# Masked attention on one Trainium2 core: key group 4 moves from TensorE's transposes to the second DMA transpose

## What is computed

```python
q, k, v = x @ Wq.T + bq, x @ Wk.T + bk, x @ Wv.T + bv
scores = q @ k.T / sqrt(128)
scores = where(adj > 0, scores, -9e15)        # adj: int32 [4096, 4096]
att = softmax(scores, axis=-1) @ v
y = x + elu(att)
out = (y - mean(y)) / sqrt(var(y) + 1e-5)
```

## Time and profile before

| | us |
|---|---|
| median of 3 runs | 428.43 (428.37 to 428.65) |
| profiled execution | 429.13 |
| its span in the profile | 427.3 |

### The profile page before, as it was taken

One profiled execution on the slowest core, in us unless ns is written; L12 is line 12 of the kernel. 1 busy time (PEld: TensorE's weight loads), 2 busy tenths in 40 slices (PEclk: granted clock), 3 DMA queues, 4 the chain that ended last, 5 costly groups with the idle time before them and its releaser, 6 DMA issues.

```text
span 427.3 us, 11462 instructions
## 1 busy us (share of the span) xinstructions
PE 416.2 (97%) x3470; PEld 311.3 (73%) x3470; DVE 360.8 (84%) x677; ACT 353.8 (83%) x742; POOL 354.0 (83%) x644
## 2 busy tenths in 40 slices
PE   7997999999999999999999999999999999999994
PEld 6764777767777777777777777777777777777784
DVE  3889988888888898888888988888889888888784
ACT  4987788888888889888888898888888988888892
POOL 0596578988898889888988898889888988898875
PEclk9999999999999999999999999999999999999999
DMA  8944999899999999999999999999999999998550
GB/s 253 399 161 111 266 275 251 208 294 263 286 268 254 275 264 267 238 280 266 259 251 280 268 265 244 272 271 263 245 277 271 256 250 271 263 267 225 104 103 21
DMA packets 149794, 104.77 MB, mean 245 GB/s; under 512 B 132755, under 2 KB 141461, under 8 KB 141717
## 3 DMA queue, kind: packets, MB, share of 16 engines
q1 hardware_dynamic: 149344, 104.41, 92.0%
q10 hardware_dynamic: 436, 0.20, 0.2%
HBM read 69.47 MB, written 2.10 MB: 167 GB/s over the span
## 4 chain that ended last, share of the span: by engine, by line
POOL 58%; issue 18%; PE 10%; DMA 4%; ACT 3%; DVE 2%; POOLq 2%; SPq 2%; ACTq 0%; DVEq 0%
POOL p_rows L409 26%; POOL res L423 5%; POOL var_eps L445 4%; POOL rstd L447 4%; POOL att_sum L416 3%; POOL y L428 3%; POOL neg_mean L434 3%; POOL att L418 3%; POOL centred L436 2%; POOL expm L425 2%; DMA p_turned<-p_rows 2%; PE ps_out L967 2%; POOL y_out L451 2%; DMA x_rows<-in_x_dram 2%; POOL var L443 1%
## 5 line engine op out<-in xcount | busy, mean ns | idle before, releaser
L409 POOL TENSOR_TENSOR p_rows<-scores,p_rows 128x256 f16<-128x256 f32 x252 | 177.0, 733 | 7.3 <-ACT p_rows L566 7.1
L696 DVE CUSTOM_DVE_ANT_0 scores<-ps_scores,adj 128x1024 f32<-128x1024 f32 x128 | 155.9, 1218 | 13.0 <-issue 9.3
L549 ACT ACTIVATE scores<-scores,neg_max 128x1024 f32<-128x1024 f32 x128 | 145.8, 1139 | 3.5 <-DVE neg_max L706 3.5
L712 DVE TENSOR_TENSOR p_lo<-ps_t,p_hi 128x512 f16<-128x512 f32 x124 | 82.6, 686 | 28.4 <-ACT p_hi L558 28.3
L682 DVE TENSOR_SCALAR adj<-adj 128x1024 f32<-128x1024 int32 x128 | 103.5, 810 | 0.2
L928 PE MATMUL ps_scores<-k_hi,q_hi 128*128 128x512 f16 x256 | 97.0, 379 | 0.5 <-DVE max_parts L696 0.5
L929 PE MATMUL ps_scores<-k_lo,q_hi 128*128 128x512 f16 x256 | 97.0, 379 | 0.0
L930 PE MATMUL ps_scores<-k_hi,q_lo 128*128 128x512 f16 x256 | 97.0, 379 | 0.0
L967 PE MATMUL ps_out<-v_parts,p_turned 128*128 128x256 f16 x496 | 95.0, 273 | 0.4 <-DMA p_turned<-p_rows 0.3
L967 PE MATMUL ps_out<-v_parts,p_hi 128*128 128x256 f16 x496 | 95.1, 273 | 0.0
L969 PE MATMUL ps_out<-v_parts,p_lo 128*128 128x128 f16 x496 | 88.5, 219 | 0.0
(11 more groups left out here) (121 smaller groups left out, 479.8 us busy)
## 6 DMA issues: line engine op xcount, KB each, us to landing
adj<-in_adj_dram SPq DMA_DIRECT2D x63, 1024.0 KB, 5.3
out_dram<-y_out SPq DMA_DIRECT2D x32, 64.0 KB, 4.9
x_rows<-in_x_dram SPq DMA_DIRECT2D x4, 256.0 KB, 4.4
x_rows<-in_x_dram SPq DMA_DIRECT2D x2, 512.0 KB, 7.6
adj<-in_adj_dram SPq DMA_DIRECT2D x2, 512.0 KB, 7.4
p_turned<-p_rows SPq DMA_TRANSPOSE x63, 4.5
w_rows<-in_L_gnn_Wq_dram ACTq DMA_DIRECT2D x1, 64.0 KB, 2.7
w_rows<-in_L_gnn_Wk_dram ACTq DMA_DIRECT2D x1, 64.0 KB, 3.3
```

What stands on the lines that cost most here:

```text
L409: last = nc.gpsimd.tensor_tensor(p_rows[c][:, w:][:, cols], s_sb[s][:, c * PIECE:c * PIECE + w][:, cols], p_rows[c][:, 0:w][:, cols], ALU. ...
L549: nc.scalar.activation(s_sb[s][:, cols], s_sb[s][:, cols], ACT.Exp, bias=neg_max[:, s:s + 1], accum_out=p_sums[:, s, c:c + 1]).then_inc(ex ...
L696: nc.vector.tensor_tensor_reduce(out=s_sb[s][:, cols], in0=ps_scores[c % 2][:, :], in1=mask_sb[s][:, cols], scale=SCALE, scalar=-3.0e38, o ...
L712: nc.vector.tensor_tensor(p_lo[:, k, :], ps_t[bank_of(s, g)][:, :], p_hi[:, k, :], ALU.subtract).then_inc(plo_ready, 1)
```

## The change

`DMA_COLS` becomes (PIECE, PIECE + BANK), so the second turn also holds group 4, with 3072 columns, and PE transposes groups 5 to 7. The high part of group 4 is a copy of its own on ACT (`high_rows_odd`, at j = 6), and its low part is made by VectorE (`low_rows_odd`, at j = 7 behind `row_max`), not by POOL. `turn` of c = 1 waits for both low parts. `high_rows` of piece 1 goes from j = 6 to j = 4. `PV_ORDER` becomes (5, 0, 1, 6, 7, 2, 3, 4). The masks are made two pieces ahead: pieces 2 and 3 of a tile at its own j = 1 and 3, pieces 0 and 1 of the next at j = 5 and 7. SP's order of DMAs stays. The rest fits prologue and epilogue to it. Cut to its core (semaphores and index changes of the last tile are left out where there is "..."):

```diff
--- before.py
+++ after.py
@@ -18,12 +18,12 @@
 EPS = 1e-5
 LOG_P_SCALE = 15.0 * math.log(2.0)
-DMA_COLS = (PIECE, PIECE)
+DMA_COLS = (PIECE, PIECE + BANK)
 BY_DMA = len(DMA_COLS)
 FIRST_PE = sum(DMA_COLS) // BANK
 PE_GROUPS = STEPS - FIRST_PE
-T_AT = {4: 6, 5: 7, 6: 8, 7: 10}
-PV_ORDER = (4, 0, 5, 6, 1, 7, 2, 3)
+T_AT = {5: 6, 6: 8, 7: 10}
+PV_ORDER = (5, 0, 1, 6, 7, 2, 3, 4)
 Q_AT = (4, 6, 7, 8, 10, 11, 12)
...
@@ -274,18 +276,26 @@
         last_ps = dict(zip(range(LAST_PE, STEPS), last_ps + [ps_t[0][:, :], ps_t[1][:, :]]))
+        LAST_ACT = 4
+
+        def turned_parts(g, s):
+
+            c = 0 if g < 2 else 1
+            first = (g - 2 * c) * BLOCKS
+            half = DMA_COLS[c] // P
+            return (p_turned[c][s][:, first:first + BLOCKS, :], p_turned[c][s][:, half + first:half + first + BLOCKS, :])
+
         def last_high(g):
             if g >= FIRST_PE:
                 return p_hi[:, g - FIRST_PE, :]
-            return p_turned[g // 2][1][:, g % 2 * BLOCKS:(g % 2 + 1) * BLOCKS, :].rearrange("p b r -> p (b r)")
+            return turned_parts(g, 1)[0].rearrange("p b r -> p (b r)")
         def last_low(g):
             if g >= FIRST_PE:
                 return p_lo[:, g - FIRST_PE, :]
-            half = DMA_COLS[g // 2] // P + g % 2 * BLOCKS
-            return p_turned[g // 2][1][:, half:half + BLOCKS, :].rearrange("p b r -> p (b r)")
+            return turned_parts(g, 1)[1].rearrange("p b r -> p (b r)")
@@ -311,6 +321,9 @@
                 sp.wait_ge(rows_lo, BY_DMA * i + c + 1)
                 sp.sem_inc(turn_begun, 1)
+                if c == 1:
+                    sp.wait_ge(rows_lo_odd, i + 1)
+                    sp.sem_inc(turn_begun, 1)
                 sp.dma_start_transpose(p_turned[c][s][:, :, :], p_rows[c][:, :]).then_inc(turned[c], 16)
@@ -405,7 +418,7 @@
                 w = DMA_COLS[c]
                 for b in range(LOW_PARTS):
-                    cols = slice(b * w // LOW_PARTS, (b + 1) * w // LOW_PARTS)
+                    cols = slice(b * PIECE // LOW_PARTS, (b + 1) * PIECE // LOW_PARTS)
                     last = nc.gpsimd.tensor_tensor(p_rows[c][:, w:][:, cols], s_sb[s][:, c * PIECE:c * PIECE + w][:, cols],
@@ -559,11 +572,18 @@
             def high_rows(i, s, c, first):
-                w = DMA_COLS[c]
                 act.wait_ge(exp_done, exp_count(i, c))
                 if not first:
                     act.wait_ge(turned[c], 16 * i)
-                nc.scalar.activation(p_rows[c][:, 0:w], s_sb[s][:, c * PIECE:c * PIECE + w], ACT.Copy).then_inc(rows_hi, 1)
+                nc.scalar.activation(p_rows[c][:, 0:PIECE], s_sb[s][:, c * PIECE:(c + 1) * PIECE], ACT.Copy).then_inc(rows_hi, 1)
+
+            def high_rows_odd(i, s, first):
+
+                act.wait_ge(exp_done, exp_count(i, 2))
+                if not first:
+                    act.wait_ge(turned[1], 16 * i)
+                nc.scalar.activation(p_rows[1][:, PIECE:PIECE + BANK], s_sb[s][:, 2 * PIECE:2 * PIECE + BANK],
+                                     ACT.Copy).then_inc(rows_hi_odd, 1)
@@ -611,8 +631,10 @@
                     if j == (1 if not warm and p == 1 else 2) and has_1:
                         high_rows(p - 1, 1 - n, 0, not warm and p == 1)
-                    if j == (3 if not warm and p == 1 else 6) and has_1:
+                    if j == (3 if not warm and p == 1 else 4) and has_1:
                         high_rows(p - 1, 1 - n, 1, not warm and p == 1)
+                    if j == (5 if not warm and p == 1 else 6) and has_1:
+                        high_rows_odd(p - 1, 1 - n, not warm and p == 1)
                     if warm and j % 2 == 1 and has_1:
@@ -631,7 +653,6 @@
                 for n in range(2):
                     period(2 * pair + n, n)
-            high_part(LAST - 1, 0, 5, False)
             exp_piece(LAST, 1, 0, False)
@@ -712,6 +733,13 @@
                                         ALU.subtract).then_inc(plo_ready, 1)
+            def low_rows_odd(i, s):
+
+                w = DMA_COLS[1]
+                dve.wait_ge(rows_hi_odd, i + 1)
+                nc.vector.tensor_tensor(p_rows[1][:, w + PIECE:2 * w], s_sb[s][:, 2 * PIECE:2 * PIECE + BANK],
+                                        p_rows[1][:, PIECE:w], ALU.subtract).then_inc(rows_lo_odd, 1)
+
             def reciprocal(i, s):
...
@@ -782,18 +810,20 @@
                     if j == 7 and has_scores:
                         row_max(p, n)
+                    if j == 7 and has_1:
+                        low_rows_odd(p - 1, 1 - n)
                     if j == 1 and has_2:
                         reciprocal(p - 2, n)
...
                         for c in ((1,), (2, 3), (), ())[j // 2] if j % 2 == 1 else ():
                             mask_piece(0, 0, c)
-                        for c in ((), (), (0,), (1, 2))[j // 2] if j % 2 == 1 else ():
+                        for c in ((), (), (0,), (1,))[j // 2] if j % 2 == 1 else ():
                             mask_piece(1, 1, c)
                     elif has_scores:
-                        if j == 1:
-                            mask_piece(p, n, 3)
-                        if j in (3, 5, 7) and makes_mask:
-                            mask_piece(p + 1, 1 - n, j // 2 - 1)
+                        if j in (1, 3):
+                            mask_piece(p, n, 2 + j // 2)
+                        if j in (5, 7) and makes_mask:
+                            mask_piece(p + 1, 1 - n, j // 2 - 2)
                     if j in rows_at:
@@ -830,16 +860,15 @@
             period(TILES - 2, 0)
             period(TILES - 1, 1, makes_mask=False)
-            low_part(LAST - 1, 0, 5)
             reciprocal(LAST - 1, 0)
             for g in (6, 7):
                 late_high_part(g)
                 low_part(LAST - 1, 0, g)
-            for g in range(LAST_PE, FIRST_PE):
+            for g in range(LAST_PE, LAST_ACT):
                 last_high_part(g)
                 last_low_part(g)
             reciprocal(LAST, 1)
-            for g in range(FIRST_PE, STEPS):
+            for g in range(LAST_ACT, STEPS):
                 last_low_part(g)
@@ -948,7 +977,7 @@
                 if g >= FIRST_PE:
                     pe.wait_ge(plo_ready, PE_GROUPS * i + g - FIRST_PE + 1)
-                elif g % 2 == 0 or pv_count(0, g - 1) > pv_count(0, g):
+                elif g in (0, 2):
                     pe.wait_ge(turned[g // 2], 16 * i + 16)
@@ -962,8 +991,7 @@
                         low = p_lo[:, g - FIRST_PE, b * P:(b + 1) * P]
                     else:
-                        high = p_turned[g // 2][s][:, g % 2 * BLOCKS + b, :]
-                        low = p_turned[g // 2][s][:, DMA_COLS[g // 2] // P + g % 2 * BLOCKS + b, :]
+                        high, low = (part[:, b, :] for part in turned_parts(g, s))
                     nc.tensor.matmul(ps_out[s][:, 0:2 * D], high, v_parts[:, k, :],
...
@@ -1029,17 +1057,16 @@
                     period(2 * pair + n, n)
             transposes(LAST - 1, 0, 6, False)
-            values(LAST - 1, 0, 4, False)
+            values(LAST - 1, 0, 5, False)
             values(LAST - 1, 0, 0, False)
             values(LAST - 1, 0, 1, False)
             transposes(LAST - 1, 0, 7, False)
-            values(LAST - 1, 0, 5, False)
             values(LAST - 1, 0, 6, False)
             last_transposes(2)
             last_transposes(3)
-            for g in (7, 2, 3):
+            for g in (7, 2, 3, 4):
                 values(LAST - 1, 0, g, False)
-            for g in range(FIRST_PE, STEPS):
+            for g in range(LAST_ACT, STEPS):
                 last_transposes(g)
```

More of the change, by code:

```diff
@@ L173, in attention_kernel @@
         rows_lo = sem("rows_lo")
+        rows_hi_odd = sem("rows_hi_odd")
+        rows_lo_odd = sem("rows_lo_odd")
         turned = [sem(f"turned{c}") for c in range(BY_DMA)]
@@ L734, in last_low_part @@
             def last_low_part(g):
-                if g < FIRST_PE:
+                if g < LAST_ACT:
                     dve.wait_ge(last_hi_dve, g - LAST_PE + 1)
                 else:
-                    dve.wait_ge(last_hi_act, g + 1 - FIRST_PE)
+                    dve.wait_ge(last_hi_act, g + 1 - LAST_ACT)
                 nc.vector.tensor_tensor(last_low(g), last_ps[g], last_high(g), ALU.subtract).then_inc(last_plo, 1)
@@ L975, in last_transposes @@
                 if g > 5:
-                    pe.wait_ge(plo_ready, PE_GROUPS * (LAST - 1) + g - FIRST_PE + 1)
+                    pe.wait_ge(plo_ready, PE_GROUPS * LAST)
                 for b in range(BLOCKS):
```

## The result

The changed kernel takes 456.47 us (455.62 to 456.85, 4 runs) against 428.54 in the same session: 27.9 us more, a ratio of 1.065 (1.0636 to 1.0663). The forecast was 437.0 (+8.6) with a range of 422 to 448, so the sign was right and the size too small by a factor of three.

What follows compares the result with a forecast made beforehand. The DMA queue was to bound the kernel at 12.46 us a tile: 28 x (12.46 - 12.20) = +7.3, plus 1.3 for an early backlog, on 428.4 gives 437.0 us, range 422 to 448.

Steps and rivals of the forecast that it cites:

- The bound: DMA queue: at 12.46 us a tile it becomes the bound, above PE's 11.77 and POOL's 11.91.
- PE's saving: PE: one group of transposes less, -0.43 us a tile, real but not seen behind the queue.
- The added bytes: Second turn: 0.262 MB more at 289 GB/s adds 0.91 us a tile to the DMA queue.
- The slack: DMA queue of the old kernel: 12.20 - 11.55 = 0.65 us a tile free, from a stretch at 278 GB/s.
- The loop: Single p_rows buffer, from landing through ACT, VectorE and SP to next landing: 11.9 to 12.2 us, below the queue.
- the landing: Second turn, from issue to arrival in p_turned: 4.4 + 0.9 = 5.3 us.
- the added wait: SP before the second turn, for VectorE's subtraction: turn issued about 0.8 us later, hidden below the queue's bound.
- The backlog term: Stretch up to 91 us: backlog no longer worked off in slack, +1.3 us in all.
- The end: Last tile: PE's -0.43 against a longer last second turn, +0.9 half hidden: 0, with 0.5 to either side.
- A: Rival: queue not the limit, POOL's 11.91 us a tile decides, -8 us to 420.4; chance 0.18.
- B: Rival: queue and loop both come out at 12.2 us a tile, no change at 428.4; chance 0.09.
- C: Rival: addition costs 1.23 us, queue and loop partly add up, from 12.9 a tile, +20 to 448; chance 0.13.

Runs made afterwards that it cites:

- e3: The kernel before with 1024 unused columns more in the second turn, group 4 staying on PE: 451.97 us, ratio 1.055.
- e7: The kernel before with 512 unused columns more in the second turn: 436.62 us, ratio 1.0188.
- e16: The kernel before with 1536 unused columns more in the second turn: 463.91 us, ratio 1.0843.
- the volume runs: The kernel before with 512, 1024 or 1536 unused columns more in the second turn: 436.62, 451.97 and 463.91 us.
- e15: The kernel before with 512 unused columns more in each of the two turns: 452.91 us, ratio 1.0586.
- e1: The changed kernel with two buffers for the second turn's rows, so ACT's copy waits for the turn of two tiles before: 454.99 us, ratio 1.061.
- e6: The changed kernel with two buffers for the second turn's rows and VectorE's subtraction ahead of the masked piece at j = 7: 452.70 us, ratio 1.0579.
- e10: The kernel before with 1024 unused columns more in the second turn and both adjacency loads together behind it: 443.66 us, ratio 1.0351.
- e5: The changed kernel with adjacency loads of half the width from the third tile on, 1.05 MB less a tile: 440.82 us, ratio 1.028.

## Why the prediction was right or wrong

**The bound**, right: the queue took over from PE and POOL, the turn holds SP for over 4 us, PE and ACT have waits for p_turned. PE's saving of 0.43 us a tile bought nothing, as forecast: e3, which keeps group 4 on PE, is no slower than the changed kernel. SP's waits fell from 2.0 each, though not to nearly nothing: 1.0 for VectorE's rows and 0.6 for POOL's, a tile. The rate over whole tiles is 265 GB/s, not the 275 to 282 that was to be its sign.

**The added bytes**, right in size: 0.91 us was forecast, and the line through e7, e3 and e16 rises by 0.83 for 1024 columns. An estimate from the Trainium skill's 261 GB/s for a transposing DMA (DMA: Bandwidth & Descriptors, Latency and other measured facts) is 1.0, from its 350 to 400 about 0.7; the measured price lies between.

**The slack**, wrong, and this is the step that failed. The forecast read "the DMA queue has 12.20 - 11.55 = 0.65 us of slack a tile" from one stretch at 278 GB/s. e7 shows that 512 unused columns, priced at 0.45 us and so well inside such a slack, already cost 8.1 us; the volume runs leave 0.1 to 0.2 of it. The kernels in which the queue decides (e3, e7, e15, e16, e1, e6, the changed one) move 265 to 271 GB/s from 150 to 390 us (e10 with its other order, 276); the old kernel moved 263 over the same stretch and was nearly full. The stretch chosen began behind a stall and so left out its price: while SP issues the turn of 71.53 the queue nearly stops for 3 us. Begun earlier, at 78.20, just behind the stall, the same trace gives 272 GB/s, 11.8 us a tile instead of 11.55. Over the five tiles from the store at 69.23 to that at 130.97, with the stall in them, it gives 261, no more than the steady stretch:

```profile
74.00:77.00 3.00, 3.00 (x28) 2.29 (x26) 2.06 (x5) 3.00 (x7) 2.92 (x6) 1.00 0.49 56
78.20:125.30 47.10, 46.71 (x394) 34.26 (x393) 40.41 (x75) 39.56 (x83) 41.03 (x72) 1.00 1.04 272
69.23:130.97 61.74, 61.35 (x521) 45.43 (x520) 53.37 (x100) 52.09 (x111) 54.17 (x96) 1.00 1.06 261
```

The 272 without the stall is still above what any of these in the old order of transfers held from 150 to 390 us. What made those tiles of the old kernel quicker, and what stopped the queue at 74, stays open. Of the 19.5 us by which the result passes the forecast, this is most: the 26 tiles lost 21.5 where the forecast gives them 26 x (12.46 - 12.20) = 6.8, so 14.7 more. In e3, bytes alone, the tile rose by 13.00 - 12.22 = 0.78 instead of 0.26.

**The loop** was priced at 11.9 to 12.2; e5 shows 12.5. Its steps were right (6.9 against 6.6), the landing wasn't: 5.5 in e5, whose queue moves only 195 GB/s, 6.5 as a median in the changed kernel.

```profile
L327 SPq DMA_TRANSPOSE p_turned<-p_rows x39: 4008/4417/5000, 147.7 to 396.1; - x39
...
DMA to landing us min/median/max: 5.5/6.5/7.0
```

It was right that it lies under the queue. That it would cost nothing there was not: together with the added wait it costs about 4 us, 456.5 against e6's 452.7.

**The backlog term**, +1.3, had the right idea and too small a number: the stretch up to the first store lost 5.7 us. After 1.3 for it and 0.5 for its tiles that is 3.9 more of the 19.5. The end, put at 0, lost 0.6.

**Rivals.** A and B are excluded by the time. C named 448 and more, from 12.9 a tile, and the result lies there, but for the wrong reason in the main: the addition was not dearer and VectorE's subtraction took 0.69. Only C's smaller part, that loop and wait add to the queue, is seen, as the 4 us above. Its size was luck.

## What to carry to other kernels

A queue shared by loads and turns is full when its rate over many tiles is what it reaches in a kernel that never lets it idle; here the waits of the issuing engine (2.0 us before each turn) and the time between issue and landing (4.4 us) didn't show that. Test it with bytes that nobody uses: e3 alone gives 452 of the 456.5 us. A best stretch taken out of a trace must start before the stall that it recovers from: 278, 272 and 261 GB/s come from one trace by where the window begins and ends.

## What the runs showed that I had not expected

A turn in one queue nearly stands still beside a load in another: 79 packets of 256 B beside 78 of 8 KB in 2 us, against 2158 without the load, and kernels 15% to 30% slower. And how long a turn holds SP tells of the queue: the first turn, which did not grow, holds SP 4.9 us at 206.01, where the old kernel's turns hold it 2.9 in the middle and 5.2 at 71.53, around its own stall.
